# Storing the results of two batches together: one DMA of 2 MB in rows of 16 KB in place of two of 1 MB in rows of 8 KB

## The reference

```python
W = weights[condition]                       # (64, 128, 128), picked from 16
x = x + einsum('bct,bcd->bdt', x, W)         # conditioned channel mixing
Bx = einsum('bni,bri->bnr', x, B[adapter])   # rank 16, picked from 64 adapters
x = x + einsum('bnr,bor->bno', Bx, A[adapter])
```

## Time and profile before

| | us |
|---|---|
| median of 3 runs | 393.79 |
| lowest and highest of them | 390.11, 395.64 |
| the profiled execution, time | 395.34 |
| its span (first to last instruction) | 393.5 |

### The profile page before, as it was taken

How to read it: one execution, slowest core, us unless ns; L and a number is a source line. 1 busy time by engine, 2 the same in 40 slices (tenths; PEclk the granted TensorE clock), 3 DMA queues, 4 the chain that set the end, 5 groups by cost and what they waited for, 6 DMA issues and landing times.

```text
span 393.5 us, 16869 instructions
## 1 busy us (share of the span) xinstructions
PE 376.5 (96%) x6170; PEld 354.3 (90%) x6170; DVE 230.8 (59%) x447; ACT 238.4 (61%) x579; POOL 112.2 (29%) x260
## 2 busy tenths in 40 slices
PE   7989989999999999999999999999999999999981
PEld 7979979999999999999999999999999999999871
DVE  0226762676555667755566775556677555667763
ACT  1566644666656666665666666566666666666541
POOL 2122330333332223333222333322233332223210
PEclk9999988999999999999999999999999999999996
DMA  7999997999999999999999999999999999999567
GB/s 272 417 362 347 407 409 277 345 415 386 406 414 412 408 416 415 415 404 414 404 418 410 416 405 410 414 405 409 414 415 414 410 406 406 415 403 413 223 250 277
DMA packets 28383, 152.24 MB, mean 387 GB/s; under 512 B 3153, under 2 KB 3154, under 8 KB 12242
## 3 DMA queue, kind: packets, MB, share of 16 engines
q1 hardware_dynamic: 28226, 151.79, 96.1%
q10 hardware_dynamic: 144, 0.26, 0.2%
HBM read 84.94 MB, written 67.11 MB: 386 GB/s over the span
## 4 chain that ended last, share of the span: by engine, by line
PE 93%; DMA 2%; issue 2%; ACT 1%; DVE 1%; POOL 1%; SPq 0%; POOLq 0%; DVEq 0%; ACTq 0%
PE bank L388 60%; PE bank L428 16%; PE bank L404 16%; DMA x_in<-in_x 2%; POOL z_pair L218 0%; ACT x_out L300 0%; DVE x_out L319 0%; ACT z_all L268 0%; POOL z_all L223 0%; ACT ft L256 0%; DVE z_pair L335 0%; DVE z_part L312 0%; DVE z_all L339 0%; SPq L134 0%; SPq L133 0%
## 5 line engine op out<-in xcount | busy, mean ns | idle before, releaser
L388 PE MATMUL bank<-m_sel,x_in 128*128 128x128 f32 x2048 | 240.8, 279 | 2.9 <-ACT ft L256 1.7
L388 PEld LDWEIGHTS bank<-m_sel,x_in 128*128 128x128 f32 x2048 | 234.1, 194 | 8.6 <-DVE x_out L319 2.7
L256 ACT COPY ft<-bank 128x512 f32<-128x512 f32 x256 | 146.1, 587 | 65.5 <-PE bank L388 63.5
L319 DVE TENSOR_TENSOR x_out<-bank,ft 128x512 f32<-128x512 f32 x253 | 154.3, 681 | 19.6 <-PE bank L428 19.5
L218 POOL TENSOR_TENSOR z_pair<-z_part 16x128 f32<-16x128 f32 x126 | 54.2, 446 | 217.0 <-DVE z_part L312 198.6
L312 DVE COPY z_part<-bank 16x128 f32<-16x128 f32 x126 | 36.2, 287 | 121.2 <-PE bank L404 119.2
L268 ACT COPY z_all<-z_all 16x128 f32<-16x128 f32 x189 | 56.0, 296 | 46.9 <-POOL z_all L223 43.8
L428 PE MATMUL bank<-z_all,at 16*128 16x128 f32 x2048 | 70.0, 282 | 2.8 <-issue 1.8
L428 PEld LDWEIGHTS bank<-z_all,at 16*128 16x128 f32 x2048 | 63.2, 187 | 10.1 <-issue 10.0
L404 PE MATMUL bank<-ft,ab_in 128*16 128x128 f32 x2048 | 65.6, 274 | 1.6 <-issue 1.6
L404 PEld LDWEIGHTS bank<-ft,ab_in 128*16 128x16 f32 x2048 | 51.4, 96 | 10.6 <-issue 5.1
(11 more groups left out here) (7 smaller groups left out, 0.9 us busy)
## 6 DMA issues: line engine op xcount, KB each, us to landing
x_in<-in_x SPq DMA_DIRECT2D x63, 1024.0 KB, 11.3
out<-x_out SPq DMA_DIRECT2D x62, 1024.0 KB, 10.1
ab_in<-in_lora SPq DMA_DIRECT2D x64, 256.0 KB, 10.0
out<-x_out SPq DMA_DIRECT2D x3, 512.0 KB, 4.3
w_all<-in_weights SPq DMA_DIRECT2D x1, 1024.0 KB, 4.9
x_in<-in_x SPq DMA_DIRECT2D x2, 512.0 KB, 6.9
out<-x_out SPq DMA_DIRECT2D x1, 256.0 KB, 4.6
out<-x_out ACTq DMA_DIRECT2D x1, 256.0 KB, 5.9
```

The costliest lines, as they stand in the source:

```text
L256: nc.scalar.copy(ft[k][u][:], bank[f_bank_of(kind, i, u, final)][:]).then_inc(copied, 1)
L319: nc.vector.tensor_tensor(x_out[k][:, UNIT * u:UNIT * (u + 1)], bank[banks[u]][:], ft[k][u][:], ALU.add).then_inc(added, 1)
L388: last = nc.tensor.matmul(to[:, P * c:P * (c + 1)], x_in[k][:, UNIT * u + P * c:UNIT * u + P * (c + 1)], m_sel[k][:], start=(c == 0), stop ...
```

## The change

The four output buffers `x_out0` to `x_out3` of 128 x 2048 become two of 128 x 2 x 2048; slot k is now a view of one half of buffer k // 2, and the rows of a pair's two batches lie side by side. The output in memory gets the same form: 32 pairs of 128 x 2 x 2048, so that a partition's 16 KB are contiguous, and the host swaps the axes back. In the loop one store of 2 MB moves a pair, after all eight adds. There are two `stored` semaphores, one for each kind, in place of four, and VectorE waits for the one of the pair. In the last turn the pairs 56/57 and 58/59 are stored jointly; batches 60 to 63 are stored as before, in pieces, into their half of the 16 KB rows.

```diff
-        x_out = [sbuf(f"x_out{k}", [P, TIME]) for k in range(BODY)]
+        x_out2 = [sbuf(f"x_out{kind}", [P, ROUND, TIME]) for kind in range(KINDS)]
+        x_out = [x_out2[k // ROUND][:, k % ROUND, :] for k in range(BODY)]
...
-        stored = [sem(f"stored{k}") for k in range(BODY)]
+        stored = [sem(f"stored{kind}") for kind in range(KINDS)]
...
-            def store(k, b):
-                sp.wait_ge(added, UNITS * (b + 1))
-                sp.dma_start(out[b], x_out[k][:]).then_inc(stored[k], 16)
+            def store(kind, r):
+                sp.wait_ge(added, UNITS * ROUND * (r + 1))
+                sp.dma_start(out[r], x_out2[kind][:]).then_inc(stored[kind], 16)
...
                     if begun(b - BODY):
-                        for i, k in enumerate(slots):
-                            store(k, b - BODY + i)
+                        store(kind, KINDS * q + kind - KINDS)
...
-                sp.dma_start(out[b, :, cols], x_out[b % BODY][:, cols]).then_inc(stored[b % BODY], 16)
-
-            for k in range(BODY - 2):
-                store(k, BATCHES - BODY + k)
+                sp.dma_start(out[b // ROUND, :, b % ROUND, cols], x_out[b % BODY][:, cols]).then_inc(stored[1], 16)
+
+            for i in range(ROUND):
+                b = BATCHES - BODY + i
+                sp.wait_ge(added, UNITS * (b + 1))
+                sp.dma_start(out[b // ROUND, :, i, :], x_out[i]).then_inc(stored[0], 16)
...
-            act.wait_ge(stored[BODY - 1], 16 * (TURNS - 1))
+            act.wait_ge(stored[1], 16 * (TURNS - 1))
...
-                    dve.wait_ge(stored[k], 16 * turns)
+                    dve.wait_ge(stored[k // ROUND], 16 * turns)
...
-    out = nc.dram_tensor("out", (BATCHES, P, TIME), F32, kind="ExternalOutput").ap()
+    out = nc.dram_tensor("out", (BATCHES // ROUND, P, ROUND, TIME), F32, kind="ExternalOutput").ap()
...
-    turned = result.results[0]["out"].reshape(BATCHES, P, CHUNKS, CHANNELS)
+    turned = result.results[0]["out"].transpose(0, 2, 1, 3).reshape(BATCHES, P, CHUNKS, CHANNELS)
```

More of the change, by code:

```diff
@@ L192, in _ @@
             store_part(BATCHES - 1, (0,))
[L193 to L196, removed]
+            sp.wait_ge(stored[0], 16 * (TURNS - 1 + 2))
+            sp.wait_ge(stored[1], 16 * (TURNS - 1 + 5))
         @block.gpsimd
@@ L302, in _ @@
             cols = slice(UNIT * (UNITS - 1), TIME)
-            act.dma_start(out[BATCHES - 1, :, cols], x_out[BODY - 1][:, cols]).then_inc(stored[BODY - 1], 16)
+            act.dma_start(out[BATCHES // ROUND - 1, :, 1, cols], x_out[BODY - 1][:, cols]).then_inc(stored[1], 16)
         @block.vector
```

## The result

The changed kernel takes 395.31 us in the median of 20 runs (391.99 to 398.33); the kernel before, run beside it on the same chip, 392.72 us (390.11 to 395.64, 20 runs). The ratio is 1.006, with a 95% interval of 1.0032 to 1.0089: slower by 0.6%, some 2.4 us (2.6 us between the medians), and not by 2%. The profiled execution took 396.64 us with a span of 394.8 us. (The 393.79 us shown ahead of the prediction was the median of the first three runs of before.)

What follows compares the result with a forecast made beforehand. TensorE was taken as the bound, with the DMA engines nearly as full. A lag 1.0 us shorter left a tail wait of +1.0 us; with 0.3 for a possible load wait, 393.79 became 395.1 us, range 390.3 to 400.0.

Steps and rivals of the forecast that it cites:

- a wait at 368.35: TensorE near the end, waiting for a batch's load if the lag grows: 0 to 2.2 us, taken as 0.3.
- TensorE bounds: Whole kernel: TensorE is busy 96% of the span, and in the middle nothing else matters while inputs and free banks arrive.
- When stores start.: Loop: a round's first 1 MB enters the DMA queue 2.4 us later, adding 2.4 us once to the lag, bounds 0 to 2.4.
- nothing else moves: Loop: apart from the first 1 MB entering the queue 2.4 us later, issues keep their times; loads are not later.
- How many packets.: Loop: nine fewer packets a round per DMA engine save 2.2 us of lag, plus 1.2 us if packets slow the engine.
- The lag: One of 16 DMA engines falls behind by 0.47 us a round; the change was to shorten this by 1.0 us at the end.
- What waits for a store.: Tail: batch 60's adds wait for both stores of pair 56/57, delaying TensorE's batch 61 product to 378.9, +1.0 us.
- C: Rival, slower by more than 2%: the lagging DMA engine becomes the bound, beyond TensorE's 18 us slack; about 403 us, chance 0.09.
- D: Rival: each 16 KB row is moved as two 8 KB packets, costing about 4.4 us; 398 us, chance 0.06.
- B: Rival, no effect: the lag shrinks by 2 us or more, or is less outside the profile; 393.8 us, chance 0.32.
- The 2.0 us for a transfer: DMA: the skill's fixed time per transfer, taken as latency already overlapped; by the page alone the sum would be 0.

Runs made afterwards that it cites:

- pair layout, two stores: The kernel before with the output in memory laid out by pairs, two 1 MB stores at the old times: 390.96 us, ratio 0.9981.
- joint, 8 KB rows: The changed kernel with memory laid out batch by batch, so the one 2 MB store has 8 KB rows: 394.87 us, ratio 1.0033.
- last pairs split: The changed kernel with batches 56 to 59 stored one by one, each on its own semaphore: 394.95 us, ratio 1.0035.
- nearly without the first stores: The changed kernel storing only 16 columns of the first batch of pairs 0 and 1, SP's loop begun one turn later: 390.03 us, ratio 0.9938.
- the control with the shorter rounds: The changed kernel with only SP's and VectorE's loops begun one turn later: 392.89 us, ratio 1.0015.

## Why the prediction was right, and where it was right for the wrong reason

**The number.** 395.1 us was forecast and 395.31 measured, and that they lie so near is luck. The +1.0 us stood for a wait that did not come, and the +0.3 for a wait at 368.35 that did not come either. The start, 393.79, was 1.1 us too high (392.72 over 20 executions), and the loss was 2.6 us between the medians, from a place that the prediction does not name.

**TensorE bounds, and the four engines' instructions cost nothing new.** Right: 249.63 of 250 us busy in the middle.

**"When stores start."** Right on the facts: only the first store of a round moves, by 2.4 us, and the landing times near 70 us are 1.9 us longer (7.6 against 5.7). That the stores make them longer is not shown: the kernel with only the last pairs late has 8.1 there with the stores of before, in a profile without the first pause. The step that failed is the sentence that nothing else moves.
| kernel | stores of batches 0 to 3 | at 0.989 or more |
|---|---|---|
| before, three groups | early | 57 of 99 |
| pair layout, two stores | early | 7 of 12 |
| only the last pairs late | early | 7 of 12 |
| after | late | 1 of 20 |
| all stores late | late | 1 of 12 |
| joint, 8 KB rows | late | 2 of 12 |
| last pairs split | late | 0 of 10 |
| only the first ones late | late | 1 of 12 |
| nearly without the first stores | left out | 8 of 12 |
| early ends, late middle, joint, both loops begun later | early | 11 of 18 |
| the same with 8 KB rows | early | 3 of 12 |
| before, both loops begun later | early | 1 of 12 |
| after, both loops begun later | late | 1 of 12 |

With SP's loop alone begun later, or neither, the early and the late stores part cleanly; where VectorE's loop too begins later they don't. The mean clock also counts the tail: the profile with only the last pairs late has 0.984 and no first pause.

So the runs show that two late stores in the first rounds cost about 3 us in the kernel of before. The way there is argued. The clock fell behind the first pause in eleven of the twelve profiles that have it (0.70 or 0.85 in 54:65.5) and in neither of the two without it, but their lengths do not go with late stores (1.76 to 2.31 us late, 1.47 to 2.58 early). How the data and the block get in each other's way, if that is it, stays open.

**"How many packets."** The count was right, the price without effect: the kernel with late 8 KB stores has the same landing times (14.9 against 15.0) as after. The lag did end lower than before, by 2.5 us rather than by 1.0, but with the late issue and not with the rows. Why was not found, and that a single DMA engine lags was not tested.

**"What waits for a store."** This term, +1.0 us, measured 0 in after's profile: the pair landed at 374.67, 0.8 us before the adds begin at 375.43, for which they wait on TensorE's product anyway. The mechanism exists, as the control with the shorter rounds shows, at 1.1 us on VectorE and 0.4 us on TensorE. It was mis-sized because the landing was taken as 16.3 us less 1.0 and was 13.4.

**The rivals.** C did not come, the landings stayed under 18 us. D did not. B was half right: the lag shrank by 2.5 us and the tail's wait vanished, yet the time rose for a reason that no rival had. The sentence that the spread of the runs "shows that something other than the schedule differs" was the clue; it should have been followed to the stage from 54 to 65.5 us, whose clock of 0.70 stood in the table by stage.

The Trainium skill, "DMA: Bandwidth & Descriptors", section "Rules for kernel authors", advises to coalesce many small transfers into large ones. From 1 to 2 MB this case shows no gain: late stores of 2 x 1 MB took 395.51 us and joint ones 395.31. The 2.0 us for a transfer that the prediction takes from the section "Anatomy of one DMA" of the same page are fitted there to DMAs that GpSimd issues; here SP issues them, so the 1.9 us of this case are a like figure for another path.

## What to carry to other kernels

Before moving transfers, look in the chain for pauses of the bound engine that nothing explains, for instruction blocks in the DMA view, and at the granted clock of the stretch behind: here two stores that began 2.4 us later, ahead of such a place, cost about 3 us. In this kernel the transfers near the first pass through the loop were best left early. A joint store is a later store; test its lateness apart from its size. And where the times of executions spread by more than an effect, compare many executions and their mean clocks, not one profile of each.

## What the runs showed that was not expected

- Two stores of 1 MB, 2.4 us late, cost 3 us (394.77 against 391.77 us; ratio 1.0063). A pause and a lower clock stand right behind them; with VectorE's loop begun later the cost does not show (1.0015 against 1.0037).
- With late stores in the loop x_in lands after 15 to 16 us at its end, with early ones after 16.0 to 19.1 us. In the three profiles at 18.4 us and more TensorE waits 0.7 to 1.3 us for loads there.
- Beginning VectorE's loop one turn later takes TensorE's waits of 0.2 us in every second round away, in all four kernels that have it; with early ends and a late middle ten of 18 executions are faster than any of before, though the median gains only 0.2% in the larger of the two runs. How the unrolled turn does this stays open.
